# A gated attention block with experts: the probability transposes a step later, the second head transposes in the scores' bank, and GpSimd rounding a tile's inputs

## The reference

```python
def _div_clamp_fp8(x, scale):
    y = jnp.clip(x.astype(jnp.float32) / scale, -448, 448)
    return _fp8_roundtrip(y.astype(jnp.bfloat16).astype(jnp.float32))

ln_out = _ln(layernorm(x), ln_w, ln_b)
q  = _ln(fp8_linear(ln_out, wq))    # 16 heads of 128
k  = _ln(fp8_linear(ln_out, wk))    # 8 groups
v  = fp8_linear(ln_out, wv)
core = softmax(q k^T / sqrt(128)) v
qx = _ln(fp8_linear(ln_out, wqx))   # and kx, vx from ctx
xout = softmax(qx kx^T / sqrt(128)) vx
x = x + tanh(g0) * (quantised(cat(core, xout)) @ wproj) * scales
x = x + tanh(g1) * moe(layernorm(x))   # 16 experts, top 2, one shared
```

## Time and profile before

| what | value |
|---|---|
| median of 3 executions | 525.98 us (520.98 to 527.2) |
| the profiled execution's time | 521.2 us |
| span of the profiled execution | 519.4 us |
| mean granted TensorE clock | 0.948 |
| PE busy | 429.8 us, 83% of the span |
| PE weight loads busy | 311.9 us, 60% |
| DVE busy | 374.1 us, 72% |
| ACT busy | 287.9 us, 55% |
| POOL busy | 233.5 us, 45% |

### The profile page before, as it was taken

How to read it: one execution, slowest core, us unless ns; L and a number is a source line. 1 busy time by engine, 2 the same in 40 slices (tenths; PEclk the granted TensorE clock), 3 DMA queues, 4 the chain that set the end, 5 groups by cost and what they waited for, 6 DMA issues and landing times.

```text
span 519.4 us, 9936 instructions
## 1 busy us (share of the span) xinstructions
PE 429.8 (83%) x2982; PEld 311.9 (60%) x2982; DVE 374.1 (72%) x846; ACT 287.9 (55%) x610; POOL 233.5 (45%) x387
## 2 busy tenths in 40 slices
PE   0587746989999999999999999999988689999930
PEld 0455525666666666666666666666667477788720
DVE  5977652698888889889888888988777853233245
ACT  3587842666756766676666766577764032323320
POOL 1253250543564365354555446443542173166660
PEclk9888985999999999999999999999999879999985
DMA  8910099999800000000000000000057033343307
GB/s 211 304 73 1 1 129 254 279 315 270 227 0 0 0 0 0 0 0 0 0 0 0 0 0 0 0 0 1 3 214 333 1 107 98 87 123 116 106 20 242
DMA packets 34811, 45.66 MB, mean 88 GB/s; under 512 B 3035, under 2 KB 32224, under 8 KB 33889
## 3 DMA queue, kind: packets, MB, share of 16 engines
q1 hardware_dynamic: 26656, 35.61, 22.5%
q0 software_dynamic: 6992, 9.46, 8.3%
q10 hardware_dynamic: 1136, 0.27, 0.3%
HBM read 28.34 MB, written 24.32 MB: 101 GB/s over the span
## 4 chain that ended last, share of the span: by engine, by line
PE 53%; issue 11%; ACT 10%; POOL 10%; DVE 8%; DMA 7%; SPq 1%; ACTq 1%; POOLq 0%; DVEq 0%
PE proj_ps L847 11%; PE score_ps L870 9%; PE headT_ps L861 6%; PE proj_ps L1000 5%; PE pv_ps L892 5%; PE proj_ps L839 5%; PE out_ps L902 4%; POOL rot L519 4%; ACT qT L669 4%; DMA wp_sb<-in_wpT 3%; ACT kT L669 2%; POOL reg L525 1%; PE pv_ps L803 1%; DMA arena<-zbuf 1%; DVE arena L1176 1%
## 5 line engine op out<-in xcount | busy, mean ns | idle before, releaser
L847 PE MATMUL proj_ps<-arena 128*128 128x512 f16 x384 | 102.1, 390 | 11.1 <-DMA wp_sb<-in_wpT 10.7
L1216 DVE BATCH_NORM_STATS2 st<-rot 128x6 f32<-128x256 f32 x192 | 72.8, 420 | 47.4 <-ACT rot L635 46.1
L635 ACT ACTIVATE rot<-proj_ps 128x512 f32<-128x512 f32 x96 | 56.7, 590 | 57.0 <-PE proj_ps L847 53.2
L861 PE MATMUL headT_ps<-idf,rot 128*128 128x128 f32 x384 | 59.5, 277 | 22.2 <-ACT qT L669 15.3
L519 POOL TENSOR_TENSOR rot<-rot,cw 128x512 f32<-128x512 f32 x64 | 70.6, 1124 | 2.5
L861 PEld LDWEIGHTS headT_ps<-idf,rot 128*128 128x128 f32 x384 | 43.3, 140 | 46.8 <-issue 33.2
L870 PEld LDWEIGHTS score_ps<-kT,qT 128*128 128x128 f32 x512 | 62.6, 196 | 7.8 <-ACT qT L669 5.3
L525 POOL TENSOR_TENSOR reg<-reg,rinv 128x512 f32<-128x512 f32 x32 | 33.4, 1045 | 73.2 <-DVE rinv L1236 73.2
L870 PE MATMUL score_ps<-kT,qT 128*128 128x64 f32 x512 | 63.2, 278 | 0.1
L847 PEld LDWEIGHTS proj_ps<-arena 128*128 (+1 forms) x384 | 37.9, 104 | 37.4 <-issue 14.7
L669 ACT ACTIVATE qT<-headT_ps,colv 128x512 f32<-128x512 f32 x64 | 49.7, 777 | 12.5 <-PE headT_ps L861 10.9
(11 more groups left out here) (215 smaller groups left out, 749.8 us busy)
## 6 DMA issues: line engine op xcount, KB each, us to landing
zbuf<-fill SPq DMA_DIRECT2D x1, 16576.5 KB, 61.8
arena<-in_wffn SPq DMA_DIRECT2D x4, 1536.0 KB, 13.5
arena<-zbuf SPq DMA_DIRECT2D x32, 128.5 KB, 2.1
wkv_stage<-in_wkvN SPq DMA_DIRECT2D x1, 2048.0 KB, 14.9
wp_sb<-in_wpT POOLq DMA_DIRECT2D x1, 2048.0 KB, 15.6
wp_sb<-ybuf SPq DMA_DIRECT2D x8, 256.0 KB, 4.9
xs<-in_x SPq DMA_DIRECT2D x2, 512.0 KB, 5.0
wp_sb<-in_wqN POOLq DMA_DIRECT2D x1, 1024.0 KB, 12.4
```

The lines of the kernel that those rows point to most:

```text
L635: act.activation(raw[c % 2][i], proj_ps[i % 2][:, :], ACT.Copy).then_inc(proj_evac, 1)
L847: mm = pe.matmul(ps, lhs, w[kind][:, ch, 512 * b:512 * b + 512], start=(k == 0), stop=(k == 3))
L861: mm = pe.transpose(dst, raw[c % 2][i][:, h * D:(h + 1) * D], idf[:, :])
L1216: ins = ve.bn_stats(st[:, 4 * i + h:4 * i + h + 2, :].rearrange("p h s -> p (h s)"), raw[c % 2][i][:, h * D:(h + 2) * D].rearrange("p (h d ...
```

## The change

Five edits, all in the attention part:

1. The second head transposes of a step go to `score_ps` instead of `headT_ps`, and wait for DVE's subtraction of the step's scores (`sub_done`) in place of ACT's copy. The third head transposes wait for the copy of the first. ACT copies the second from `score_ps`.
2. Probability transposes of a step move from between the second and third head transposes to the following step, after bank 0 and ahead of the scores.
3. ACT's copy of them moves along, to a place after the evacuation of bank 0.
4. DVE does the first three of the five operations on the next tile's inputs (`inputs_magnitude`), into a buffer `xm` of its own.
5. POOL does the addition and the subtraction (`inputs_round`) in step c2, after the norm banks and, in n=2, ahead of `load_output_weights`. Tile 0 keeps all five on DVE.

```diff
@@ -184,6 +184,7 @@
         ya = sb("ya", [P, 1024], BF16)
         ym = sb("ym", [P, 1024], F16)
         ys = sb("ys", [P, 1024], F16)
+        xm = sb("xm", [P, XW], F16)
 
         mx = sb("mx", [P, 8], F32)
         sm = sb("sm", [P, 8], F32)
@@ -492,6 +493,15 @@
                 ins.then_inc(sem, 1)
                 gp.wait_ge(sem, count)
 
+            xin16 = xin[:, :].bitcast(F16)
+
+            def inputs_round(T):
+
+                gp.wait_ge(xmag_done, T + 1)
+                gp.tensor_tensor(xin16, xin[:, :], xm[:, :], ALU.add).then_inc(xbig_done, 1)
+                gp.wait_ge(xbig_done, T + 1)
+                gp.tensor_tensor(xq[:, bass.ds(T * XW, XW)], xin16, xm[:, :], ALU.subtract).then_inc(xgrid_done, 1)
+
             def variance(n, x):
 
                 gp.wait_ge(bn_done, n + 1)
@@ -539,6 +549,8 @@
                     norm_bank(n, c, 2)
                 if c == 0 and live(n, -NU):
                     inputs_over_scale(t + 1)
+                if c == 2 and live(n, -NU):
+                    inputs_round(t + 1)
                 if isinstance(n, int) and n == 2:
                     load_output_weights()
 
@@ -666,7 +678,8 @@
                     dst = qT[:, c % 2, 4 * (b % 2):4 * (b % 2) + 4, :]
                 else:
                     dst = kT[:, c % 2, :, :]
-                act.activation(dst, headT_ps[:, :].rearrange("p (h t) -> p h t", h=4), ACT.Identity,
+                ps = (headT_ps, score_ps, headT_ps)[i]
+                act.activation(dst, ps[:, :].rearrange("p (h t) -> p h t", h=4), ACT.Identity,
                                scale=col(kind + "w"), bias=col(kind + "b")).then_inc(headT_evac, 1)
 
             def expo(w, s):
@@ -685,6 +698,8 @@
                     evacuate(n, c, 0)
                 for j in next_folds(n, 0):
                     fold_high(j)
+                if live(n, 3):
+                    prob_copy(n - 3, (c - 3) % 2)
                 if heads:
                     norm_bank0(n - 1, before)
                 if proj:
@@ -705,8 +720,6 @@
                     fold_high(j)
                 if heads:
                     heads_out(n - 1, before, 1)
-                if attend:
-                    prob_copy(n - 2, c % 2)
                 if heads:
                     heads_out(n - 1, before, 2)
                 if proj:
@@ -851,13 +864,17 @@
 
             def head_transposes(n, c, i):
                 pe.wait_ge((norm0_done, norm1_done, norm2_done)[i], n + 1)
-                ge(pe, headT_evac, 3 * n + i)
+                if i == 1:
+                    ge(pe, sub_done, n)
+                else:
+                    ge(pe, headT_evac, 3 * n + (0, 0, 1)[i])
+                ps = (headT_ps, score_ps, headT_ps)[i]
                 for h in range(4):
                     if i > 0:
-                        dst = headT_ps[:, :].rearrange("p (g b h s) -> p g b h s", g=2, b=2, h=2)\
+                        dst = ps[:, :].rearrange("p (g b h s) -> p g b h s", g=2, b=2, h=2)\
                             [:, h // 2, :, h % 2, :]
                     else:
-                        dst = headT_ps[:, h * P:(h + 1) * P]
+                        dst = ps[:, h * P:(h + 1) * P]
                     mm = pe.transpose(dst, raw[c % 2][i][:, h * D:(h + 1) * D], idf[:, :])
                 mm.then_inc(headT_done, 1)
 
@@ -955,6 +972,8 @@
                     project(t, c, 0)
                 for j in next_folds(n, 0):
                     fold(j)
+                if live(n, 3):
+                    prob_transposes(n - 3, (c - 3) % 2)
                 if attend:
                     scores(n - 2, c % 2)
                 if isinstance(n, int) and n == NU * NT + 1:
@@ -981,8 +1000,6 @@
                     fold(j)
                 if heads:
                     head_transposes(n - 1, before, 1)
-                if attend:
-                    prob_transposes(n - 2, c % 2)
                 if heads:
                     head_transposes(n - 1, before, 2)
                 if isinstance(n, int) and n == NU - 1:
@@ -1196,9 +1213,15 @@
                     wait_free()
                 ve.tensor_tensor(q, ys[:, :], ym[:, :], ALU.subtract).then_inc(grid, 1)
 
-            def inputs_to_grid(T):
+            def inputs_magnitude(T):
+
                 ve.wait_ge(xin_done, T + 1)
-                to_grid(xin[:, :], xq[:, bass.ds(T * XW, XW)], (xclip_done, xabs_done, xmag_done, xbig_done, xgrid_done), T)
+                ve.tensor_scalar(xin[:, :], xin[:, :], FP8_MAX, -FP8_MAX, ALU.min, ALU.max).then_inc(xclip_done, 1)
+                ve.wait_ge(xclip_done, T + 1)
+                ve.tensor_scalar(xm[:, :].bitcast(U16), xin[:, :].bitcast(U16), 0x7FFF, None,
+                                 ALU.bitwise_and).then_inc(xabs_done, 1)
+                ve.wait_ge(xabs_done, T + 1)
+                ve.tensor_scalar(xm[:, :], xm[:, :].bitcast(BF16), 128.0, 3.0, ALU.mult, ALU.max).then_inc(xmag_done, 1)
 
 
             in3 = xin[:, :].rearrange("p (j c t) -> p j c t", j=4, c=HC)
@@ -1206,7 +1229,11 @@
             ve.tensor_tensor(in3, xT[:, :, 0:P].unsqueeze(1).to_broadcast([P, 4, HC, P]),
                              sinv[:, :].rearrange("p (j c) -> p j c", j=4).unsqueeze(3)
                              .to_broadcast([P, 4, HC, P]), ALU.mult).then_inc(xin_done, 1)
-            inputs_to_grid(0)
+            inputs_magnitude(0)
+            ve.wait_ge(xmag_done, 1)
+            ve.tensor_tensor(ys[:, :], xin[:, :], xm[:, :], ALU.add).then_inc(xbig_done, 1)
+            ve.wait_ge(xbig_done, 1)
+            ve.tensor_tensor(xq[:, 0:XW], ys[:, :], xm[:, :], ALU.subtract).then_inc(xgrid_done, 1)
             for j in range(2, NFOLD):
                 fold_low(j)
 
@@ -1285,7 +1312,7 @@
                 if live(n, 3):
                     quantise(n - 3, (c - 3) % NU)
                 if proj and c == 1 and live(n, -NU):
-                    inputs_to_grid(t + 1)
+                    inputs_magnitude(t + 1)
                 if c == 3 and live(n, NU):
                     residual(t - 1)
 
```

## The result

| what | before | after |
|---|---|---|
| median | 523.48 us (520.48 to 527.2) | 497.56 us (494.47 to 499.4) |
| ratio after / before | | 0.950, 95% interval 0.940 to 0.959 |
| profiled execution, its span | 521.2, 519.4 us | 494.47, 492.6 us |
| mean granted clock | 0.948 | 0.947 |

The change takes 26.8 us off the span, 8.4 more than the 18.4 forecast. The direction and the range (494 to 517) held. The time lies close to the third rival (waits vanish nearly wholly, 495.5), though not by that rival's terms (see "Rivals").

What follows compares the result with a forecast made beforehand. PE and DVE were nearly full, with PE waiting about 4.6 us per tile. Span 519.4 - 17.7 - 1.9 + 2.4 - 1.2 = 501.0 us, plus 1.8 around it and a good microsecond for scatter: 504 us, range 494 to 517.

Steps and rivals of the forecast that it cites:

- the third rival: Whole kernel: waits vanish nearly wholly, no collisions, rounding at 1.9 us, tile 38.8, total 495.5 us; chance 0.17.
- What bounds the kernel: Loop tile: PE and DVE nearly full; PE waits about 4.6 us of 42.65, its work without waits taking 38.1.
- The tile: Loop and last tile: new tile 39.7 us, saved 2.95 each, six tiles -17.7 us.
- (a): Second head transposes into score_ps: scores wait for qT 0.45 us in c1, about 0.3 in c0, nothing in c2, c3.
- (b): Probability transposes and copy one step later: their 0.21 us wait in c2 goes; POOL's normalisation gains a wide margin.
- (c): Two DVE operations to POOL: 2.03 us each, DVE loses 1.97 a tile; c0's scores and first-bank wait together 0.5.
- (d): DVE and POOL collisions: 0.3 us in c2 and 0.4 in c0, bounds 0 and 1.05 for each.
- (e): First loop tile, 81.8 to 128.4 us: same waits go, less transposes now after the DMA stall, -1.9 us.
- (f): Output weights' load: issue slips 4.1 us behind the rounding, POOL arrives 1.7 earlier, +2.4 us; bounds 1.4 and 3.4.
- (g): Tail: last third transposes gain, last probability copy is exposed by 0.85 us, DVE's serial chain moves earlier, -1.2 us.
- The first: Loop, c2 and c0: ACT's queue keeps PE waiting, tile 41.1, total 512 us; chance 0.16.
- The second: Next tile's first bank: POOL becomes the bound, gain gone at 3.5 us per operation, 528 at 4.1; chance 0.05.

Runs made afterwards that it cites:

- the split version: Kernel after with POOL's addition in c1, subtraction in c2, and the output weights' load issued ahead of both and of the variances: 484.41 us, ratio 0.919.
- the bank alone: Kernel before with only the second head transposes moved to the scores' bank; probability transposes, their copy and DVE's five operations unchanged: 527.87 us, ratio 1.004.
- bank and POOL: Kernel after with the probability transposes and their copy back in their old place: 518.61 us, ratio 0.984.
- the first experiment: Kernel after with POOL's rounding taken back, DVE doing all five input operations, new orders on PE and ACT kept: 508.57 us, ratio 0.966.
- the load first: Kernel after with the output weights' DMA issued ahead of POOL's rounding in step n=2: 495.32 us, ratio 0.937.
- bank and late: Kernel after with all five input operations on DVE again, the second bank and late probability transposes kept: 508.57 us, ratio 0.966.
- the rounding in c1: Kernel after with POOL's rounding (addition and subtraction) one step earlier, in c1 instead of c2: 499.29 us, ratio 0.946.
- order_only: Kernel after with all five input operations back on DVE, only the new orders on PE and ACT staying: 508.57 us, ratio 0.966.
- three operations: Kernel after with a third, unused operation of the same size on POOL between addition and subtraction: 536.05 us.
- the clock kept up: Kernel after with a third, unused POOL operation, plus ten unused matmuls on PE ahead of the next tile's first bank: 519.99 us, ratio 0.989.
- late alone: Kernel before with only the probability transposes and their copy moved one step later; one bank, inputs on DVE: 535.02 us, ratio 1.019.

## Why the prediction was right, and where it was off

**What bounds the kernel: right.** The waits were the gain. The work without waits was put at 38.1 us a tile, and the split version shows 38.15.

**The tile: -17.7 forecast, -20.07 measured** (five and the last), by its own terms:

- *(a) Scores waiting for qT, 0.45 in c1.* 0.19 measured. I added ACT's durations (0.69, 0.78, 0.78), but the operations start 0.59 and 0.66 us after one another (247.97, 248.56, 249.22), the end of one overlapping the next. The start-to-start way that I used for PE was not used for ACT.
- *(b) The wait of the probability transposes goes, POOL's normalisation gains a wide margin.* Right, and more weighty than I said: with the bank alone this wait is 2.02 us and brings the half clock; with bank and POOL it is 8.8 us in six waits. I costed the late transposes nearly at nothing; on top of the other two edits they are worth 1.84 us a tile (40.96 to 39.12).
- *(c) POOL's operations at 2.03 each, and a wait of 0.5 for them.* 2.13 and 0.55 measured. The Trainium skill, GPSIMD Engine Reference, would give 2.25 by estimate from its measured 4497 ns for 2048 f32 elements (section 3.1) and advises against the move (section 4.1). The rows of 2.13 are below that, and the move pays here: 40.78 a tile with all on DVE, 39.12 with two on POOL.
- *(d) Collisions at 0.7 a tile.* The rows lengthened as forecast (DVE 1.15 beside POOL 2.39), and in c2 they cost PE nothing: kT comes 0.19 us before it is wanted. I had given room for 1.9 us of insertion and then charged 0.7 within that room. Here the sum is off, 0.7 for 0. Had the insertion been the old five operations, it would have run over: that is the 0.71 + 1.19 of the first experiment.

So 39.7 was 0.6 too high, of which (d) is 0.7 and (a) 0.3, with small amounts the other way: the normalisation 0.3 late for the first late transposes in c0.

**(e) First tile: -1.9 forecast, -6.08 measured.** The step that failed: I counted waits and left out the clock. Behind the DMA's stall PE runs at half rate, and it took longer to be back at full rate in the kernel before. Windows of before and after:

```profile
81.80:86.00 4.20, 4.17 (x17) 3.27 (x17) 0.76 (x2) 1.76 (x5) 0.00 (x0) 0.50 0.91 302
86.00:90.00 4.00, 4.00 (x21) 2.61 (x22) 1.91 (x4) 1.11 (x2) 0.00 (x0) 0.50 1.09 328
```

```profile
81.30:86.00 4.70, 4.69 (x23) 3.68 (x24) 0.76 (x2) 2.36 (x6) 0.00 (x0) 0.61 0.92 302
86.00:92.00 6.00, 6.00 (x51) 4.26 (x51) 4.10 (x9) 2.98 (x5) 1.28 (x3) 1.00 1.11 297
```

By the durations at either rate this is about 2.2 us of the 6.1 (an estimate). Another 3.5 are what every loop tile saved (42.59 to 39.12), of which I had counted 1.9. The last 0.4 I can't place. That the 2.2 us belong to the change is not shown: after stalls of nearly one length, 11.8 to 11.9 us, the first step takes 11.95 us with the load first, 9.87 with bank and late, and 9.25 with the rounding in c1.

**(f) The weights' load: +2.4 forecast, -0.52 measured.** The rounding did push the issue back, by 4.2 us: in the kernel after the norm banks of n=2 end at 61.00 and the load is issued at 65.24. What I mis-sized is how much sooner these norm banks come. They start at 58.96 instead of 63.81, 4.85 us sooner, where I took 1.7 (bounds 0.7 to 2.7). Part of it is again the clock, in a step I had not priced. The timeline of before, then of after:

```profile
45.34 0.63 PE L861 MATMUL headT_ps<-idf,rot 128*128 128x128 f32 x4 [1.72 <-ACT qT L669]
45.80 2.71 PE L839 MATMUL proj_ps<-arena 128*128 128x512 f16 x6
...
63.81 2.04 POOL L519 TENSOR_TENSOR rot<-rot,cw 128x512 f32<-128x512 f32 x2
```

```profile
43.41 1.46 PE L852 MATMUL proj_ps<-arena 128*128 128x512 f16 x6
...
58.96 2.04 POOL L529 TENSOR_TENSOR rot<-rot,cw 128x512 f32<-128x512 f32 x2
```

A wait of 1.72 us for the one bank was followed by a bank of 2.71 us. Without the wait the bank takes 1.46.

**(g) Tail: -1.2 forecast, -0.13 measured.** From the last cut to the last scores 0.87 us were won (9.65 to 8.78), and behind them 0.74 lost (124.55 to 125.29). I made no run for it alone, and the cause is open.

**The range held partly by luck.** (e) missed by 4.2 us and (f) by 2.9, both the same way, and (f) lies outside its own bounds. The median of 497.56 is inside 494 to 517, but the profiled execution, at 494.47, is only 0.5 above the lower end.

**Rivals.** The third came nearest, through the collisions that cost nothing. Its terms are not those measured: it had -23.1 for the six tiles, -2.5, -1.5 and +1.4, and the trace gives -20.07, -6.08, -0.13 and -0.52; and its rounding at 1.9 us took 2.13. The first (ACT's queue keeps PE waiting) did not come about, since the second operation is off DVE: order_only's 40.78 is what it looks like. The second (POOL the bound) is nearer than I put it. At 2.13 us each the wait is 0.55. I set the point from which the gain is gone at 7 us for both operations. With 6.4 us on POOL (three operations) the traced tile was already at 44.49 against 42.64 before, since the wait brought the half clock with it; with the clock kept up the same 6.4 us gave 41.20.

## What to carry to other kernels

Here three edits that alone cost a little or gain nothing are worth 8% of a loop together, since each wait removed uncovers the one queued behind it: price a change by what each engine's queue will wait for next, and test the combinations, not the parts. Put work moved to another engine where that queue has a gap as long as the piece, in pieces if need be, and issue DMAs ahead of it. Price a chain of operations from start to start, and look at the granted clock after every stall of PE, not only at the stall.

## What the runs showed of the hardware

- A PE wait in a busy loop can cost more than its length: 2.71 us of wait had 3.3 us more behind it at 1.2 GHz in the traced execution (tile 44.49 against 41.20), 2.02 us had 1.2 on average, with a fall in four tiles of five, and 0.71 + 1.19 us brought a fall in two c2 steps of six. Waits of 1.46 us once a tile (bank with POOL) and 19 waits of about 0.95 us in five tiles (late alone) brought none. The same 1.99 us did in one kernel and not in another.
- Behind the long stall for the DMA, the slow stretch was not longer for a longer stall: idle 16.4 us, first step 9.75; idle 11.8, first step 11.95; idle 5.2 (split version), 9.26. Nor does one length of stall give one stretch: behind 11.8 to 11.9 us of idle the granted clock stays at 0.50 for about 8 us with the load first, and for under 4 with bank and late and with the rounding in c1 (first steps 11.95, 9.87 and 9.25). What decides it is open.
- A two-input f16/bf16 operation of 1024 elements takes POOL 2.13 us in the loop of the kernel after. In the kernel with the third operation it is 2.30 where DVE's absolute value falls into it, and that one then takes 2.22 us instead of 0.43. A pair of norm banks takes it 2.04 alone, and 2.39 beside one DVE operation, which itself takes 1.15 there, against a mean of 0.43 for that operation in the kernel before.
- Behind the last scores the kernel before and the one after take 124.6 and 125.3 us in the first measurement, and the same kernel after takes 128.5 in its second. Whether that goes with the chip, as I had expected, is not shown, but it makes a ratio to a kernel measured elsewhere unsafe.
